# A hybrid attention kernel, its linear phase: beginning rearranged, x of tile 1 turned at once, and a projection that waits for the low parts of u one by one

## What is computed

```python
x = x + attn_a(layernorm(x), wq, wk, wv, wo)      # causal softmax attention with rope, one head
x = x + ffn(layernorm(x), W_r, W_k, W_v, mu_r, mu_k)
x = x + attn_b(layernorm(x), Wq, Wk, Wv, Wf, Wb, A_log, dt_bias, Wg, bg, Wo, norm_w)
x = x + ffn(layernorm(x), W_r, W_k, W_v, mu_r, mu_k)
```

```python
q, k = l2norm(silu(x @ Wq)), l2norm(silu(x @ Wk))
v, g = silu(x @ Wv), sigmoid(x @ Wf - dt_bias)
beta, A = sigmoid(x @ Wb), exp(-exp(A_log))
o_t   = (q_t @ state) * g_t
state = A * state + beta_t * outer(k_t, v_t)
o = rmsnorm(o) * norm_w * sigmoid(x @ Wg + bg)
return o @ Wo
```

## Time and profile before

| | |
|---|---|
| median of 3 runs | 904.65 us (904.13 to 906.27) |
| profiled execution, its own time | 908.08 us |
| its span, first to last instruction | 906.0 us |
| mean granted clock of TensorE | 0.974 |
| TensorE, matmuls | 824.8 us busy, 91% |
| TensorE, weight loads | 711.7 us, 79% |
| GpSimd | 584.4 us, 65% |
| ScalarE | 569.4 us, 63% |
| VectorE | 554.9 us, 61% |
| first FFN / linear phase begins / its steady steps | 235.7 / 281.0 / from about 360, some 34 us each |

### The profile page before, as it was taken

One profiled execution on the slowest core, in us unless ns is written; L12 is line 12 of the kernel. 1 busy time (PEld: TensorE's weight loads), 2 busy tenths in 40 slices (PEclk: granted clock), 3 DMA queues, 4 the chain that ended last, 5 costly groups with the idle time before them and its releaser, 6 DMA issues.

```text
span 906.0 us, 31429 instructions
## 1 busy us (share of the span) xinstructions
PE 824.8 (91%) x13280; PEld 711.7 (79%) x13280; DVE 554.9 (61%) x1296; ACT 569.4 (63%) x1202; POOL 584.4 (65%) x514
## 2 busy tenths in 40 slices
PE   4858998999797799999999999999999999997877
PEld 3647997899695687888788788888888888885776
DVE  3976566567684356557467467467467467566473
ACT  4746554665565666767767767767767766754544
POOL 4983211320455788977977977977977977986322
PEclk9988999999997899999999999999999999997999
DMA  5001000100100000000000000000000000000011
GB/s 190 26 12 36 25 13 1 31 18 2 25 1 1 1 3 3 4 3 3 3 3 3 4 3 3 4 3 3 4 2 3 3 3 3 3 3 2 13 31 51
DMA packets 19417, 12.38 MB, mean 14 GB/s; under 512 B 7760, under 2 KB 18768, under 8 KB 19024
## 3 DMA queue, kind: packets, MB, share of 16 engines
q1 hardware_dynamic: 19280, 10.39, 4.0%
HBM read 8.29 MB, written 2.10 MB: 11 GB/s over the span
## 4 chain that ended last, share of the span: by engine, by line
PE 50%; DVE 9%; POOL 4%; issue 3%; ACT 2%; DVEq 0%; POOLq 0%; ACTq 0%
PE la_ps L1465 7%; PE la_ps L1467 6%; PE la_ps L1466 6%; DVE la_u_lo L1773 4%; PE la_o_ps L1528 4%; PE la_o_ps L1544 4%; PE la_s_ps L1558 4%; PE la_ps L1575 3%; PE la_ps L1509 3%; DVE la_u L1767 3%; PE la_ps L1609 2%; PE la_ps L1496 2%; PE la_ps L1610 2%; PE la_ps L1611 2%; PE la_ps L1598 1%
## 5 line engine op out<-in xcount | busy, mean ns | idle before, releaser
L2109 POOL TENSOR_TENSOR la_coef<-la_ssk,lt_mhalf 128x32 f32<-128x32 f32 x16 | 87.1, 5442 | 71.2 <-DVE la_ssk L1784 71.2
L1465 PE MATMUL la_ps<-la_x_hi,w_hi 128*128 128x256 f32 x384 | 116.7, 304 | 2.0 <-ACT la_v L1924 1.0
L1467 PE MATMUL la_ps<-la_x_hi,w_lo 128*128 128x256 f32 x384 | 107.6, 280 | 0.1
L1466 PE MATMUL la_ps<-la_x_lo,w_hi 128*128 128x256 f32 x384 | 107.5, 280 | 0.0
L2141 POOL TENSOR_TENSOR la_scale<-la_scale,lt_mhalf 128x32 f32<-128x32 f32 x16 | 99.9, 6241 | 6.7 <-DVE la_scale L1760 6.4
L1807 DVE TENSOR_TENSOR lt_state<-la_s_ps,la_faded 128x512 f32<-128x512 f32 x62 | 42.6, 687 | 70.6 <-PE la_o_ps L1544 57.5
L1465 PEld LDWEIGHTS la_ps<-la_x_hi,w_hi 128*128 128x128 f32 x384 | 72.4, 189 | 14.5 <-issue 6.2
L713 ACT ACTIVATE at_probs<-at_s_ps,at_ntop 128x512 f32<-128x512 f32 (+2 forms) x80 | 49.0, 623 | 46.5 <-DVE at_ntop L655 46.4
L598 PE MATMUL at_o_ps<-V,at_probsT 128*128 128x128 f32 x544 | 74.6, 277 | 3.2 <-DVE at_probsT L507 2.0
L531 POOL CAST at_q_hi<-qk_hi 128x128 fp32r<-128x128 f32 x32 | 9.4, 294 | 104.9 <-PE at_s_ps L572 102.4
L598 PEld LDWEIGHTS at_o_ps<-V,at_probsT 128*128 128x128 f32 x544 | 69.1, 192 | 6.5 <-ACT at_probsT L729 2.3
(11 more groups left out here) (216 smaller groups left out, 2501.3 us busy)
## 6 DMA issues: line engine op xcount, KB each, us to landing
at_w_raw<-in_w SPq DMA_DIRECT2D x20, 128.0 KB, 2.2
X<-in_x SPq DMA_DIRECT2D x8, 256.0 KB, 2.9
out<-X SPq DMA_DIRECT2D x8, 256.0 KB, 2.3
qkv_cos<-in_cos SPq DMA_DIRECT2D x1, 1024.0 KB, 5.0
qkv_sin<-in_sin SPq DMA_DIRECT2D x1, 1024.0 KB, 7.2
lt_w_out<-in_w_out SPq DMA_DIRECT2D x4, 128.0 KB, 2.7
const<-in_const SPq DMA_DIRECT2D x1, 320.5 KB, 3.3
qkv_w<-in_w_qkv SPq DMA_DIRECT2D x1, 320.0 KB, 3.9
```

What stands on the lines that cost most here:

```text
L1465: eng.matmul(out, l_hi, r_hi, start=True, stop=False)
L1466: eng.matmul(out, l_hi, r_lo, start=False, stop=False)
L1467: return eng.matmul(out, l_lo, r_hi, start=False, stop=True)
L2109: eng.tensor_tensor(coef[:, :], ssk[:, :], mhalf[:, :], ALU.pow).then_inc(s["coef_step"], 1)
```

## The change

- **FFN, norm of the first two tiles.** first_vector is cut into first_moments and first_normalized. VectorE takes the moments at the end of slot 6, GpSimd makes the roots in slot 6, VectorE normalizes at the start of slot 7.
- **FFN, GpSimd.** tables.gpsimd_clear and gpsimd_selectors go from the linear phase into slot 7, behind gpsimd_strict.
- **Linear phase, VectorE.** tables.vector goes from slot 8 of the FFN to the head of VectorE's stream; ScalarE therefore waits for w_ready 3, and betas(0) for the loads themselves.
- **Linear phase, ScalarE.** One Silu of a single column at the head of its stream.
- **x of tile 1.** Its turning, copies and low part go from the end of step -1 to behind betas(0), beta_tanh(0) and the head of step -1, with a job x1 of its own in the ring; turned(n) names the job for each tile.
- **project_out** waits for ulo_ready before each even chunk instead of once for all four.

```diff
+    def first_moments(self, eng):
+        for k in range(2):
+            self.moments(eng, Tile(0, k))
+
+    def first_normalized(self, eng):
         for k in range(2):
             self.normalize(eng, Tile(0, k))
...
+                if next_norm is not None and g.off == GROUPS - 2:
+                    next_norm.first_gpsimd(eng)
                 if tables is not None and g.off == GROUPS - 1:
                     tables.gpsimd_strict(eng)
-                if next_norm is not None and g.off == GROUPS:
-                    next_norm.first_gpsimd(eng)
+                    tables.gpsimd_clear(eng)
+                    tables.gpsimd_selectors(eng)
...
             def slot(g):
-                if tables is not None and g.off == GROUPS:
-                    tables.vector(eng)
-                if next_norm is not None and g.off == GROUPS:
-                    next_norm.first_vector(eng)
+                if next_norm is not None and g.off == GROUPS - 1:
+                    next_norm.first_normalized(eng)
...
+                if next_norm is not None and g.off == GROUPS - 2:
+                    eng.wait_ge(x_ready, B)
+                    next_norm.first_moments(eng)
...
             if job == "xt":
-                return exists(m + 2)
+                return exists(m + 2) and m != -1
+            if job == "x1":
+                return m == -1
...
-        ring = Ring(("f0 f1 su f2 sT f3 be k0 k1 v0 v1 kT0 kT1 s10 s11 k2 k3 sq sB v2 b0 b1 b2 b3 v3 q0 q1 q2 q3 y g0 g1 yt g2 "
+        ring = Ring(("f0 f1 su f2 sT f3 be x1 k0 k1 v0 v1 kT0 kT1 s10 s11 k2 k3 sq sB v2 b0 b1 b2 b3 v3 q0 q1 q2 q3 y g0 g1 yt g2 "
...
+        def turned(n):
+
+            return n - 2, "x1" if n == 1 else "xt"
...
-                eng.wait_ge(s["ulo_ready"], 4 * m)
                 bank = free(eng, m, "y")
                 out = ps[bank][:, 0:W]
                 for c in range(NP):
+                    if c % 2 == 0:
+                        eng.wait_ge(s["ulo_ready"], 4 * (m - 1) + c // 2 + 1)
...
                 if nxt:
                     betas(m + 1)
+                if m == -1:
+                    turn_x(1)
+                if nxt:
                     by_token(m, "k0")
...
+            tables.vector(eng)
             for m in STEPS[:-1]:
                 step(m)
...
+                if m == -1:
+                    copy_x(1)
+                if nxt:
                     silu_token(m, "k0")
...
+            eng.activation(beta[:, 0:1], const[:, C_LEFT:C_LEFT + 1], ACT.Silu)
             for m in STEPS[:-1]:
                 step(m)
...
+                if m == -1:
+                    low_x(1)
                 if now:
                     decay_queries(eng, m, 0)
...
-            step(STEPS[0])
-            tables.gpsimd_clear(eng)
-            tables.gpsimd_selectors(eng)
-            for m in STEPS[1:-1]:
+            for m in STEPS[:-1]:
                 step(m)
```

More of the change, by code:

```diff
@@ L118, in first_vector @@
             self.moments(eng, Tile(0, k))
+        for k in range(2):
+            self.normalize(eng, Tile(0, k))
+    def first_moments(self, eng):
+        for k in range(2):
+            self.moments(eng, Tile(0, k))
+    def first_normalized(self, eng):
         for k in range(2):
@@ L1447, in turn_x @@
             def turn_x(n):
-                bank = free(eng, n - 2, "xt")
+                bank = free(eng, *turned(n))
                 eng.wait_ge(norm.ready, B * (n + 1))
@@ L1457, in betas @@
                 bank = free(eng, n - 1, "be")
+                if n == 0:
+                    eng.wait_ge(tables.loaded, 16 * tables.LOADS)
                 eng.wait_ge(s["xt_ready"], n + 1)
@@ L1692, in step @@
                     by_feature(m, "g3")
-                if exists(m + 2):
+                if exists(m + 2) and m != -1:
                     turn_x(m + 2)
@@ L1817, in normalize @@
             def normalize(n):
-                written(eng, n - 4, "xt")
+                written(eng, *turned(n - 2))
                 norm.normalize(eng, Tile(0, n))
@@ L1956, in high_w_out @@
             def high_w_out():
-                eng.wait_ge(tables.w_ready, 1)
+                eng.wait_ge(tables.w_ready, 3)
                 eng.activation(tables.w_out_hi[:, :, :], tables.w_out[:, :, :], ACT.Copy).then_inc(s["w_hi_ready"], 1)
@@ L1977, in copy_x @@
                     written(eng, n - 2, "be")
-                bank = written(eng, n - 2, "xt")
+                bank = written(eng, *turned(n))
                 eng.activation(xT[:, :], ps[bank][:, 0:W], ACT.Copy).then_inc(s["xt_ready"], 1)
@@ L2096, in low_x @@
                 eng.wait_ge(s["xt_ready"], n + 1)
-                taken(eng, n - 2, "xt")
+                taken(eng, *turned(n))
                 if n > 1:
```

## The result

| | before | changed |
|---|---|---|
| median of 9 runs each | 906.49 us (904.13 to 910.98) | 899.11 us (895.52 to 901.12) |
| ratio | | 0.9901, 95% interval 0.9878 to 0.9925: 9.0 us less |
| a second measurement | 905.41 us (15 runs) | 895.07 us (4 runs), 0.9881 (0.9866 to 0.9895): 10.8 us less |
| profiled execution | 908.08 us, span 906.0 | 897.68 us, span 894.5 |

The ratio is estimated over all runs and isn't that of the two medians, which differ by 7.4 and 10.3 us. The change is faster, by 9.0 us (6.8 to 11.1) and 10.8 us (9.5 to 12.1) where 12.3 were forecast, and 899.11 lies above the stated range of 889.0 to 896.5; 895.07 lies in it. Part of that is the base: the forecast was subtracted from a median of three runs, 904.65; the other medians of the kernel before are 905.4 to 906.5. The rest is in the traces.

What follows compares the result with a forecast made beforehand. TensorE was taken to set the pace, losing time to waits for u's low parts and holes at the linear phase's beginning and end. 5.8 + 3.5 + 1.8 + 1.2 = 12.3 us off median 904.65 gave 892.3, range 889.0 to 896.5.

Steps and rivals of the forecast that it cites:

- to the second recall of step 0: Beginning of the linear phase: recall starts at 313.6 instead of 319.42, 5.8 us sooner, hand-over included.
- the hand-over: FFN to linear phase: GpSimd closes the FFN, 0.9 us saved, 0.7 lost to the Silu, net 0.2 us.
- second recall to first projection: Step 1: separate waits for the low parts of u save 0.25 us, as in a steady step.
- steps 2 to 14: Steady steps: separate waits for the low parts of u save 0.25 us each.
- step 15, last projection: TensorE's last two waits for the low parts of u shrink by 1.8 us and 1.2 us.
- Part 1: project_out waits for low parts of u singly: 3.5 us in steps 1 to 14, 1.8 and 1.2 at the end.
- The dummy Silu: Start of the linear phase: its early table load makes x of tile 0 copied 0.7 us later (0.3 to 0.8).
- Rival 6: ScalarE held behind the table load as long as the load took, 1.28 us: 893.6 us; chance 0.02.
- Step 0: TensorE's 4.25 us wait for tile 1's la_x_lo goes; normalization beside GpSimd's key product is late next; recall 5.8 us sooner.
- From there all move as one: After step 0's recall, GpSimd, VectorE and ACT follow TensorE as before, so the 5.8 us gain stays.
- Rival 3: Clock falls in step 0 all the same, behind new holes of 0.5 and 1.2 us: 2.4 lost, 894.7; chance 0.08.
- Rival 1: Clock comes back sooner in step 15 behind the shorter hole: up to 2.6 us more, 889.7; chance 0.12.

Runs made afterwards that it cites:

- e7: Kernel before with only x of tile 1 turned, copied and split at once in step -1: ratio 0.9945, 5.0 us less than before.
- e1: Kernel before with only project_out's four separate waits for the low parts of u: ratio 0.9919, 7.3 us less than before.
- e3: Changed kernel with GpSimd's clear and selectors back in the linear phase, behind tile 1's low part: ratio 0.9838, 14.7 us less than before.
- e6: Changed kernel with the normalization of tiles 0 and 1 back ahead of output(6): ratio 0.9880, 10.9 us less than before.
- e11: Kernel before with the separate waits for u only in step 15 and the last projection: ratio 0.9970, 2.7 us less than before.
- e5: Changed kernel with GpSimd's clear and selectors back in the linear phase and without the first Silu: ratio 0.9858, 12.9 us less than before.
- e0: The changed kernel unaltered, measured again beside the other runs: ratio 0.9881 to the kernel before, 10.8 us less.
- e12: Repeat of e3, the changed kernel with clear and selectors back in the linear phase: ratio 0.9836, 14.9 us less than before.

## Why the prediction came out as it did

By its own terms, on the profiled executions (the forecast for them was 895.8, and 897.68 came; for the span 893.7, and 894.5):

| term | forecast | in the two profiles | what the runs say |
|---|---|---|---|
| to the second recall of step 0 | 5.8 | 4.57 | 5.8 in S by x of tile 1 (e7); the hand-over loses 1.5; the clock gives 1.0 (K) and takes 0.8 (S) |
| second recall to first projection | 0.25 | -1.22 | 0.30 (e1, e3, e6), less 1.0 to 1.5 where the clock falls, about what K had gained |
| steps 2 to 14 | 3.25 | 5.01 | 1.45 of it was lost in the profile of before alone (e11) |
| step 15, last projection | 1.8 + 1.2 | 1.34 + 2.03 | 2.7 (e11) |

That the span came within 0.8 us of its forecast is luck: steps 2 to 14 and the last projection gave 2.6 us more than their terms, for reasons that aren't theirs.

- **Part 1** held. The 0.25 us of the steady step was 0.30 to 0.33; the rows had 0.30 idle of the weight loader, and that was the better of the two readings. That e11, which changes nothing in steps 2 to 14, still gains 1.45 there on the profile of before shows how far issue gaps of a single execution reach: the 5.01 are not to be read as this term.
- **The hand-over is the step that failed.** The prediction took VectorE's end at 278.7 and made GpSimd the last, at 279.75. It weighed the moved clear and selectors as GpSimd's own time alone, 5.28 us "beside nothing that waited", and held the normalization moved into "idle time" at 0.6 us. It was idle time of VectorE, but not of the port: x_lo(7), strict and now the clear ran there without a pause. The pair of the earlier trace rows, 2.10 us beside a GpSimd product, was priced in step 0 and not asked again at the hand-over. GpSimd did end early enough (276.51 + 2.48 = 278.99); the end came from VectorE, ScalarE and TensorE behind the blocked normalization, at 281.30. So the term that failed is the hand-over's net gain of 0.2 us: F and H, from x_lo(7) to the first matmul of k0, grew by 1.5 us (0.7 at the end of the FFN, 0.8 for the Silu). With 1.7 us less, the sum of 12.3 is 10.6, near the 10.8 of the second measurement and within the interval of the first. The Trainium skill (SBUF — State Buffer, Who interferes with whom), which I applied to step 0, has the rule; the traces agree with it that the second to start blocks, and show besides that it stays blocked through operations that the other engine has queued up behind (4.76 against 2.41 us).
- **The dummy Silu** cost about what was forecast: from the last write of X to the copy of x, 1.68 us against 1.02, so 0.66 (0.7). Rival 6, a hold behind the load, is out: in e5 the activation follows the load by 0.01 us. The drain of 1380 ns that the Trainium skill gives (ScalarE: Activation LUTs, What ACT_TABLE_LOAD costs) doesn't show behind it, here or in the changed kernel, where the Silu begins at 282.87, behind 281.58 + 1.28.
- **Step 0** was read right: x of tile 1 gave 5.96 (5.6), and the next to be late was the normalization beside the key product. In the changed kernel's first profile 0.8 us more went by the fall of the clock near 298, through la_coef (1.27 us instead of 0.45), which e0 didn't lose.
- **"From there all move as one"** was wrong in step 1. TensorE has a hole of 1.82 us there in the kernel before too; I had looked for the clock only behind holes that the change touches. Rival 3 named the right mechanism at the wrong places: no fall behind the two new holes of step 0, but one near 298, ahead of step 0, in three traces (0.8 us), and one in step 1 in six (1.0 to 1.5 us, about what the early rise had given).
- **Rival 1** came true in some executions. Between the projection of step 15 and the last, e0, e3, e5 and e12 gain 4.1 us on the profile of before and the changed kernel's first profile 2.0; behind the hole their clock is 1.00 and 0.59. The same stretch of e0_after_again:

```profile
826.20:832.00 5.80, 5.74 (x68) 1.00 0.01 3
```

  With it and without it, one kernel's executions lie 2 us apart.
- **The range** added bounds for terms, but nothing for the base (0.8 to 1.8 us) and nothing for a clock that differs from execution to execution in places that the change doesn't touch (0.8 us near 298, 2.1 us behind step 15). The hand-over's bound "from 0.1 us lost" should have been 1.5.

## What to carry to other kernels

Before work is moved into an engine's idle time, look at what the engine that shares its port does there: VectorE's idle slot beside a long run of GpSimd was worth less than nothing, and moving GpSimd's own work into the same run made it worse; taking that one move back made the end of the FFN come 2.7 us sooner, and the whole time 4 us less. Put what has no deadline (memsets, selectors) where nobody on the path is near. And each hole of the pacing engine, also one that the change doesn't touch, is a place where its clock may fall: list them before writing that the rest moves as one. When two traces are compared, cut them where the clock rises and falls: the recall that came 1.3 us later in e3 than in e12 says nothing of the kernel, the stretch S behind it agrees to 0.02 us.

## What was not expected of the hardware

- A normalization of 0.34 us was blocked for 2.41 us beside one GpSimd operation and for 4.76 us where seven memsets followed that operation without a gap: it didn't get in between.
- The same hole of 1.82 us in the same kernel let the clock fall in one execution and not in another (e12 and e3: P 39.33 and 38.14). In all 13 traces with this hole it fell where the clock had come up early some 60 us before, and only there.
- Behind a table load of 1.28 us the activation began within 0.01 us.
